# A decoder layer on one core: cross attention, its projection, the norm and the experts in one program, with a token chunk's later stages woven between the attention steps of the next chunk

## The chip, the core and the metric

The kernel runs on one core of one Trainium2 chip. Its engines work from queues of their own and meet only at semaphores: TensorE (PE, with its weight loads shown apart as PEld), VectorE (DVE), ScalarE (ACT), GpSimd (POOL), and SyncE (SP), which issues all DMAs here. Each queue is worked off in the order in which it was written. The metric is the device time in microseconds of one execution; the kernel before takes 1327.97 us (median of three runs, 1327.39 to 1332.73).

## The reference, cut to what matters

One decoder layer over 2048 tokens of width 256. After causal self attention and a layer norm come the stages that this change touches:

```python
qp = x @ Wq.T                               # 16 heads of 16
mem = kv[argmax(qp @ kv.T)]                 # each token picks one of 1601 context rows
mk, mv = split(mem @ Wkv.T)                 # one key, one value, shared by the heads
attn = softmax(qh @ mk.T / 4)               # over 2048 chosen rows, many of them equal
x = layernorm(x + (attn @ mv) @ Wc.T)
probs = sigmoid(x @ router_w.T)             # 8 experts, the best 2 are kept
combine = top-2 weights, normed to sum 1, 0 for the other experts
for e in range(8):                          # widths 256 x4, 512 x4
    y += combine[:, e] * (square(relu(x @ W1[e])) @ W2[e])
x = layernorm(x + y)
```

Equal rows are counted once, so that the keys of cross attention are at most 512 with this data: four tiles of 128 keys.

## The kernel before

The tokens stand in 16 tiles of 128 or four chunks of 512 (`NC` = 4, `C` = 512, `TC` = 4 tiles in each). The program is a row of blocks; no engine starts a block before all have ended the one ahead. The last three blocks are:

1. **Cross attention** (`attention("cross", ...)`). There are 16 units: a chunk and a group of four heads (`NG` = 4, `GH` = 4). A unit has 16 *pieces*: TensorE multiplies a query tile with all 512 keys (L527) into a bank of the ring `cross_max`, and VectorE takes the row maximum (L625). From them come the negated maxima (`cross_shift`), turned by TensorE (L532) and sent by a DMA into two rows of the query stack `stackx` (L463). Then come the unit's four *steps*, one for each tile of keys: scores in two pairs (L546), Exp (L592), and the sum over keys with the values (L557). Pieces of later units stand between the steps of the present one, where `schedule` puts them; each step is cut in thirds (after the first pair of scores, after the second, after the values). After a unit its sums are copied (L604), turned back (L536) and divided (L642, L644). The queries of a whole chunk, in 6 DMAs of 256 KB, are loaded at once (L453). The 8 banks of PSUM are 4 for scores, 1 for the output, 3 for the ring.
2. **Projection and norm** (`project_norm("n2", ...)`). For each chunk: turn the attention output (L758, copied at L787), multiply it by Wc (L776), add the residual (L810), mean and variance (L813, L815, L828, L830), the root on ScalarE (L834), normalise (L840), turn again (L758) and split into two fp32r parts (L787, L802). Beside that w2 is loaded and split into two parts (ScalarE L110, GpSimd L116).
3. **Experts.** First the router for all tokens, and its top 2 as a chain of small VectorE instructions (L1309 to L1328). Then for each chunk and expert the hidden tiles of 128 columns (function `hidden`, 6 matmuls of 512 columns each, into three banks `ph`), Relu (L1275) and Square (L1277) on ScalarE, the split on VectorE (L1298, L1300); and four output tiles `y`, each 6 or 12 matmuls of 256 columns per 256 or 512 of width, into four banks `py`, added to x at L1337. The hidden tiles of the next expert stand ahead of the outputs of this one. `product` (L92) makes three matmuls of each product, first by first, first by rest, rest by first. Then the last norm, and the output.

The line that keeps a ring in order, on TensorE, is the same before and after:

```python
if n >= SB:                  # SB = 3
    pe.wait_ge(*freed[n - SB])
```

## Time and profile before

| | us |
|---|---|
| median of three runs | 1327.97 |
| the profiled execution, its own time | 1334.47 |
| its span, first to last instruction | 1332.8 |
| loading the first queries of cross attention | 753.7 to 769.4 |
| cross attention | 769.4 to 987.6 |
| projection and norm, then the router | 987.6 to 1048.1 |
| experts up to the last matmul | 1048.1 to 1325.5 |
| last norm and output | 1325.5 to 1332.8 |

All times of instructions are those of the profiled execution, counted from the start of its span. A duration of a matmul holds the filling and draining of the array, so that a long row of matmuls is shorter than the sum of its single durations: the distance between the starts of like rows says what one costs. The same holds in a smaller measure for the other engines.

### The profile page before, as it was taken

How to read it: one execution, taken by the hardware profiler on the slowest of the kernel's cores; microseconds unless marked ns; L12 is line 12 of the kernel's file. 1: busy time of each engine (PE TensorE's matmuls, PEld its weight loads, DVE VectorE, ACT ScalarE, POOL GpSimd, SP SyncE). 2: the span in 40 equal slices, each digit the busy share in tenths (PEclk: the TensorE clock that was granted, in tenths of full speed). 3: DMA queues.
4: the chain of work that ended last, by engine and by line, in shares of the span. 5: the costliest groups of instructions: out<-in, count | busy, mean ns of one | idle time of the engine just before them, and what ended most of it. 6: DMA issues, size and time to landing. Idle time of an engine off the chain costs nothing. (4 is left out here: it accounts for less than half of the span.)

```text
span 1332.8 us, 18319 instructions
## 1 busy us (share of the span) xinstructions
PE 1171.6 (88%) x6937; PEld 642.9 (48%) x6937; DVE 955.4 (72%) x1875; ACT 640.6 (48%) x870; POOL 183.7 (14%) x167
## 2 busy tenths in 40 slices
PE   5864999999999999973899479999976799999997
PEld 2531233333333333243788213333334489999997
DVE  3564999898888887027699579999808466767675
ACT  1320246666766666841443115677653334444442
POOL 2223111021021100143000340500004000000000
PEclk9875799999999999986899659999987899999999
DMA  6215067920000000030110394200011000000000
GB/s 233 93 47 105 25 72 80 111 25 1 1 1 1 1 1 2 1 133 27 48 48 1 44 99 48 96 2 2 1 47 59 1 1 1 16 1 17 1 16 17
DMA packets 43927, 51.00 MB, mean 38 GB/s; under 512 B 7002, under 2 KB 39386, under 8 KB 43834
## 3 DMA queue, kind: packets, MB, share of 16 engines
q1 hardware_dynamic: 43834, 49.78, 19.4%
q8 instruction: 57, 0.93, 0.3%
q14 instruction: 36, 0.29, 0.1%
HBM read 37.64 MB, written 11.53 MB: 37 GB/s over the span
## 5 line engine op out<-in xcount | busy, mean ns | idle before, releaser
L625 DVE TENSOR_REDUCE self_piece_max<-self_max 128x1 f32<-128x512 f32 (+3 forms) x640 | 349.4, 604 | 52.4 <-PE self_max L527 25.4
L592 ACT ACTIVATE self_probs<-self_scores 128x1024 f32<-128x1024 f32 (+3 forms) x320 | 274.1, 896 | 192.9 <-PE self_scores L546 191.9
L527 PE MATMUL self_max<-stack_k,stack_q 96*128 96x512 bf16 (+3 forms) x640 | 209.6, 366 | 12.5 <-DMA stack_k<-kparts 6.3
L625 DVE TENSOR_REDUCE cross_piece_max<-cross_max 128x1 f32<-128x512 f32 x256 | 161.4, 684 | 28.4 <-PE cross_max L527 28.0
L546 PE MATMUL self_scores<-stack_q,stack_k 98*128 98x512 bf16 (+3 forms) x640 | 170.3, 350 | 4.3 <-DMA stack_q<-self_shift 3.0
L592 ACT ACTIVATE cross_probs<-cross_scores 128x1024 f32<-128x1024 f32 x128 | 124.7, 1022 | 93.5 <-PE cross_scores L546 91.6
L557 PE MATMUL self_out<-self_probs,V 128*17 128x512 f32 (+3 forms) x1280 | 148.7, 536 | 2.6 <-ACT self_probs L592 2.0
L527 PEld LDWEIGHTS self_max<-stack_k,stack_q 96*128 96x128 bf16 x640 | 62.2, 98 | 181.2 <-DVE self_piece_max L625 131.0
L1275 ACT ACTIVATE o_tok<-ph 128x512 f32<-128x512 f32 x96 | 57.5, 599 | 143.7 <-PE ph L92 137.5
L92 PE MATMUL py<-w_first,hid_first 128*128 128x256 f32 x384 | 108.9, 283 | 5.7 <-DVE x_sb L1337 5.7
L92 PE MATMUL py<-w_first,hid_rest 128*128 128x256 f32 x384 | 108.8, 283 | 0.0
L92 PE MATMUL py<-w_rest,hid_first 128*128 128x256 f32 x384 | 108.7, 283 | 0.0
L527 PE MATMUL cross_max<-kx_few,stackx 97*128 97x512 bf16 x256 | 95.9, 418 | 13.5 <-DMA stackx<-xparts 12.9
L494 POOL TENSOR_SCALAR_AFFINE_SELECT self_probs<-self_probs 128x512 f32<-128x512 f32 x64 | 40.6, 634 | 397.7 <-ACT self_probs L592 397.4
L1337 DVE SCALAR_TENSOR_TENSOR x_sb<-py,mix,x_sb 128x256 f32<-128x256 f32 x128 | 61.7, 482 | 36.2 <-PE py L92 29.7
L1298 DVE CAST hid_first<-o_tok 128x512 fp32r<-128x512 f32 x96 | 41.0, 427 | 64.0 <-ACT o_tok L1277 61.2
L546 PEld LDWEIGHTS self_scores<-stack_q,stack_k 98*128 98x128 bf16 x640 | 57.0, 99 | 53.8 <-ACT self_probs L592 16.3
L546 PE MATMUL cross_scores<-stackx,kx_few 99*128 99x512 bf16 x256 | 77.6, 387 | 3.2 <-DMA stackx<-cross_shift 3.1
L92 PEld LDWEIGHTS py<-w_first,hid_first 128*128 128x128 f32 x384 | 73.4, 191 | 7.4 <-issue 6.1
L92 PE MATMUL ph<-x2T_first,w_first 128*128 128x512 f32 x192 | 76.2, 397 | 0.0
L92 PE MATMUL ph<-x2T_rest,w_first 128*128 128x512 f32 x192 | 76.1, 396 | 0.0
L92 PE MATMUL ph<-x2T_first,w_rest 128*128 128x512 f32 x192 | 75.7, 394 | 0.0
(209 smaller groups left out, 1756.2 us busy)
## 6 DMA issues: line engine op xcount, KB each, us to landing
stack_q<-qparts SPq DMA_DIRECT2D x96, 64.0 KB, 8.3
stackx<-xparts SPq DMA_DIRECT2D x24, 256.0 KB, 10.9
stack_k<-kparts SPq DMA_DIRECT2D x18, 256.0 KB, 13.3
qparts<-parts SPq DMA_DIRECT2D x8, 384.0 KB, 2.5
kparts<-parts SPq DMA_DIRECT2D x8, 384.0 KB, 2.5
xparts<-xparts_sb SPq DMA_DIRECT2D x8, 384.0 KB, 2.7
cross_raw<-in_w SPq DMA_DIRECT2D x4, 768.0 KB, 5.4
n_raw<-in_w SPq DMA_DIRECT2D x6, 512.0 KB, 4.2
```

What stands on the lines that cost most here:

```text
L92: ins = nc.tensor.matmul(out, lhsT[a], rhs[b], start=first and n == 0, stop=last and n == len(terms) - 1)
L494: nc.gpsimd.affine_select(out=blk, in_=blk, compare_op=ALU.is_ge, fill=0.0, base=0, pattern=[[0, GH], [1, P]], channel_multiplier=-1).then ...
L527: mm = nc.tensor.matmul(slot[:, 0:pc["w"]], pc["lhsT"], pc["rhs"], start=True, stop=not pc["diag"])
L546: mm = nc.tensor.matmul(ps[:, j, st["off"]:C], st["keys"](j), st["queries"](j), start=True, stop=True)
L557: mm = nc.tensor.matmul(po[32 * j:32 * j + VW, st["off"]:C], st["values"](j), probs[:, i % 3, j, st["off"]:C], start=st["first"], stop=st[ ...
L592: nc.scalar.activation(probs[:, i % 3, 2 * pair:2 * pair + 2, st["off"]:C], ps[:, 2 * pair:2 * pair + 2, st["off"]:C], ACT.Exp, scale=SCAL ...
L625: nc.vector.tensor_reduce(piece_max[:, u % 2, pc["row"], pc["at"]:pc["at"] + 1], slot[:, 0:pc["w"]], AX.X, ALU.max).then_inc(side_read, 1)
L1275: nc.scalar.activation(relu[:, u % 3], ph[:, u % 3], ACT.Relu).then_inc(h_read, 1)
L1298: nc.vector.tensor_copy(hid[0][:, i % 2, w], square[:, u % 3]).then_inc(first_ready, 1)
L1337: nc.vector.scalar_tensor_tensor(out=x_sb[:, n], in0=py[:, y % 4, 0:D], scalar=mix[:, n, e:e + 1], in1=x_sb[:, n], op0=ALU.mult, op1=ALU.a ...
```

## The change

The three blocks become one. Its TensorE program is still the 64 attention steps, but `merge` puts items of the later stages behind the pieces in each third of a step, as soon as the chunk that they belong to has left attention:

- `back` (turn the attention output, 2 in a chunk), `proj` (2), `stats`, `norm`, `x2t` (turn and split the normed x, 2), `logit`, `ltr` and `mix` (router), `hid` (a hidden tile, 24), `rest` (its second part, on VectorE), `y` (an output tile, 32), `fstats` and `fnorm` (last norm).
- All that TensorE makes for these items goes through the one ring of three banks that the pieces use: the item waits until the third item before it has been read, by VectorE or by ScalarE.
- The weave gives each third of a step about 3,500 matmul columns, as long as items are ready; gaps counted in columns keep items apart (`gap`, in the list `norms`; 5 x 512 columns between `hid` and `rest`, 2 x 512 between `rest` and `y`). What is left after the last step follows in a row.
- Queries are loaded by unit (6 DMAs of 64 KB) into four slots (`SX` = 4), a unit two ahead, and from the fifth unit on only when the slot's last user is done.
- The hidden tile's first part is now written by ScalarE itself, with a second Square, and VectorE's cast goes. The root of the norms is a power of -0.5 on GpSimd. All of w1 and w2 is split on GpSimd, during the first chunk's attention.
- The router runs per chunk (4 tiles), not for all 16 tiles.

The diff, cut (`schedule` is only moved):

```diff
+SX = 4
+HR = 6
-            stackx = sb(stage, "stackx", [P, NC, H, C], BF16)
+            stackx = sb(tail, "stackx", [P, SX, GH, C], BF16)
+            banks = psum(tail, "banks", [P, 8, C])
+            ps, po, pm = banks[:, 0:GH], banks[:, GH], banks[:, GH + 1:8]
+            def merge(steps, works, first_of, before, thirds, diag_before):
+                norms = [[(("back", c, 0), 0), (("back", c, 1), 0), (("proj", c, 0), 4 * C), (("proj", c, 1), 0), (("stats", c), 2 * C),
+                          (("norm", c), 16 * C), (("x2t", c, 0), 3 * C), (("x2t", c, 1), 0), (("logit", c), 6 * C), (("ltr", c), 6 * C),
+                          (("mix", c), 3 * C)] for c in range(NC)]
...
+                    if rests and (force or now - when[("hid",) + rests[0]] >= 5 * C):
+                        give(("rest",) + rests.pop(0), slot)
...
+                pace = per_chunk * NC / (len(steps) * 3)
+                for i, step in enumerate(thirds):
+                    for k, given in enumerate(step):
+                        slot = list(given)
+                        credit = min(credit + pace, 4 * pace) if out_of[0] else 0
+                        while credit > 0:
+                            had = clock[0]
+                            if not pick(slot, False):
+                                break
+                            credit -= clock[0] - had
...
+                            if item[0] == "turn":
+                                sp.wait_ge(shift_ready, u + 1)
+                                for b, dst in enumerate(works[u]["shift_to"]):
+                                    sp.dma_start(dst, shift[:, u % 2, b]).then_inc(shift_in[u % 2], 16)
+                                if u + 2 < len(works):
+                                    if u + 2 >= SX:
+                                        sp.wait_ge(probs_used, first_of[u + 3 - SX])
+                                    load_unit(u + 2)
...
+                            elif kind == "hid":
+                                for k in range(KD):
+                                    mm = product(slot, [v[:, k, w * P:(w + 1) * P] for v in w1_sb], [xt[:, k] for xt in x2T], k == 0, k == KD - 1)
...
+                                nc.scalar.activation(relu[:, h % 2], slot, ACT.Relu).then_inc(act_read, 1)
+                                nc.scalar.activation(hid[0][:, h % HR], relu[:, h % 2], ACT.Square)
+                                nc.scalar.activation(relu[:, h % 2], relu[:, h % 2], ACT.Square).then_inc(square_ready, 1)
...
-    nc = bacc.Bacc("TRN2", target_bir_lowering=False, num_devices=1)
+    nc = bacc.Bacc("TRN2", target_bir_lowering=False, num_devices=1, dynamic_dma_scratch_size=1024)
```

**First place: TensorE's queue, the projection.** Before, this is the whole second block; `n_pt` and `n_py` are its banks, and no attention is left.

```order
L758 MATMUL n_pt<-ident,o_tok 128x128 x16
L776 MATMUL n_py<-n_w,n_oT 128x256 x8
L758 MATMUL n_pt<-ident,o_tok 128x128 x8
L776 MATMUL n_py<-n_w,n_oT 128x256 x8
L758 MATMUL n_pt<-ident,x_sb 128x128 x8
```

Now the same work of chunk 0 stands in the steps of unit 4, the first unit of chunk 1 (L1502 scores, L1441 pieces, L1511 values, L1453 `back`, L1460 `proj`; `banks` is all of PSUM).

```order
L1502 MATMUL banks<-stackx,kx_few 128x512 x2
L1441 MATMUL banks<-kx_few,stackx 128x512 x2
L1453 MATMUL banks<-ident,o_tok 128x128 x8
L1502 MATMUL banks<-stackx,kx_few 128x512 x2
L1441 MATMUL banks<-kx_few,stackx 128x512
L1460 MATMUL banks<-xwc_sb,o_tok 128x256 x4
L1511 MATMUL banks<-cross_probs,vx_few 17x512 x4
```

A matmul of the projection that had only its own kind around it has now the scores, pieces and values of another chunk on both sides.

**Second place: VectorE's queue, from the norm to the router.** Before, the router's chain works on 16 tiles at once, behind the split of the first hidden tiles (`hid_first`, `hid_rest`):

```order
L840 TENSOR_SCALAR x_sb<-x_sb,n_mv,n_rstd 128x256 x4
L802 TENSOR_TENSOR x2T_rest<-n_pt,x2T_first 128x512 x4
...
L1298 CAST hid_first<-o_tok 128x512
L1300 TENSOR_TENSOR hid_rest<-o_tok,hid_first 128x512
L1309 TENSOR_SCALAR gate<-gate 128x128
L1310 RECIPROCAL gate<-gate 128x128
L1312 MAX top<-gate 128x8 x16
L1315 MAX_INDEX at<-top,gate 128x8 x16
```

Now (chunk 0) norm, split and router stand among the maxima of pieces (L1623), which TensorE's ring waits for:

```order
L1623 TENSOR_REDUCE cross_piece_max<-banks 128x1 x5
L1670 TENSOR_SCALAR x_sb<-x_sb,norm_mv,norm_rstd 128x256 x4
L1623 TENSOR_REDUCE cross_piece_max<-banks 128x1
L1675 TENSOR_TENSOR x2T_rest<-banks,x2T_first 128x512 x2
L1703 TENSOR_TENSOR hid_rest<-o_tok,hid_first 128x512
...
L1680 TENSOR_SCALAR gate<-gate 128x32
L1681 RECIPROCAL gate<-gate 128x32
L1683 MAX top<-gate 128x8 x4
L1686 MAX_INDEX at<-top,gate 128x8 x4
```

The chain is on a quarter of the tiles and comes four times, with pieces, sums and output tiles queued behind it.

**Third place: SP's queue at the start of cross attention.** Before (16x16x512 is a chunk's part of the queries, `cross_shift` the maxima):

```order
L453 DMA stackx<-xparts 16x16x512 x12
L463 DMA stackx<-cross_shift 1x16x128 [waits cross_shift_ready]
L463 DMA stackx<-cross_shift 1x16x128
L453 DMA stackx<-xparts 16x16x512 x6
```

Now (16x4x512 is a unit's part; `o_tok` holds the raw weights):

```order
L1350 DMA stackx<-xparts 16x4x512 x6
L1355 DMA xwc_sb<-in_xwc 128x2x256
...
L1369 DMA stackx<-cross_shift 1x16x128 [waits cross_shift_ready]
L1369 DMA stackx<-cross_shift 1x16x128
L1350 DMA stackx<-xparts 16x4x512 [waits cross_probs_used]
L1350 DMA stackx<-xparts 16x4x512 x5
L1377 DMA o_tok<-in_w 128x6x256 [waits w_split] x2
```

The load of a unit's queries has moved from the start of the block to behind the maxima of the unit two before it, and from the fifth unit on behind a wait for the values of a step.

## Rows read from the trace of the kernel before

**Rows 1.** The page: the span.

```profile
span 1332.8 us, 18319 instructions
```

**Rows 2.** Windows: stretches, busy time and count by engine, TensorE clock, DMA.

```profile
753.68:769.43 15.75, 2.07 (x2) 0.50 (x2) 0.17 (x1) 1.28 (x1) 15.28 (x9) 0.50 1.06 116
799.65:965.07 165.42, 163.78 (x932) 51.92 (x932) 154.28 (x285) 112.23 (x122) 19.64 (x8) 1.00 0.16 30
965.07:987.64 22.57, 19.97 (x125) 4.77 (x124) 1.92 (x6) 17.51 (x20) 0.00 (x0) 1.00 0.01 2
987.64:1048.05 60.41, 39.05 (x170) 28.89 (x169) 34.21 (x82) 18.80 (x32) 14.33 (x7) 0.77 0.19 58
1048.05:1325.54 277.49, 271.81 (x1730) 247.25 (x1728) 182.55 (x421) 121.29 (x198) 0.00 (x0) 0.98 0.02 7
```

**Rows 3.** Timeline, 881 to 887: start, length, instruction of attention's steady steps.

```profile
883.11 0.39 PE L527 MATMUL cross_max<-kx_few,stackx 97*128 97x512 bf16 x1
883.33 0.60 PE L546 MATMUL cross_scores<-stackx,kx_few 99*128 99x512 bf16 x2
...
884.94 1.05 PE L557 MATMUL cross_out<-cross_probs,vx_few 128*17 128x512 f32 x8
885.93 0.39 PE L527 MATMUL cross_max<-kx_few,stackx 97*128 97x512 bf16 x1
```

**Rows 4.** Timeline of projection and norm, with idle time and releaser.

```profile
1000.26 1.04 PE L758 MATMUL n_pt<-ident,o_tok 128*128 128x128 f32 x8
1001.13 3.62 PE L776 MATMUL n_py<-n_w,n_oT 128*128 128x256 f32 x16
1004.59 1.04 PE L758 MATMUL n_pt<-ident,o_tok 128*128 128x128 f32 x8
1010.23 2.42 DVE L840 TENSOR_SCALAR x_sb<-x_sb,n_mv,n_rstd 128x256 f32<-128x256 f32 x1
1013.04 3.78 PE L776 MATMUL n_py<-n_w,n_oT 128*128 128x256 f32 x8 [5.69 <-DVE x_sb L810]
1018.22 1.89 PE L776 MATMUL n_py<-n_w,n_oT 128*128 128x256 f32 x8
1031.38 1.38 DVE L840 TENSOR_SCALAR x_sb<-x_sb,n_mv,n_rstd 128x256 f32<-128x256 f32 x4
```

**Rows 5.** The chain that ended last: matmuls of one chunk's experts.

```profile
1197.66 2.82 PE py L92 x24
1200.48 2.77 PE ph L92 x12
...
1264.44 2.82 PE py L92 x24
```

**Rows 6.** The page's groups: busy time, mean ns, idle before.

```profile
L625 DVE TENSOR_REDUCE cross_piece_max<-cross_max 128x1 f32<-128x512 f32 x256 | 161.4, 684 | 28.4 <-PE cross_max L527 28.0
L592 ACT ACTIVATE cross_probs<-cross_scores 128x1024 f32<-128x1024 f32 x128 | 124.7, 1022 | 93.5 <-PE cross_scores L546 91.6
L1337 DVE SCALAR_TENSOR_TENSOR x_sb<-py,mix,x_sb 128x256 f32<-128x256 f32 x128 | 61.7, 482 | 36.2 <-PE py L92 29.7
```

**Rows 7.** Timeline around the router's chain on VectorE, and one Square.

```profile
1058.34 0.69 DVE L1300 TENSOR_TENSOR hid_rest<-o_tok,hid_first 128x512 fp32r<-128x512 f32 x1
1058.95 0.22 DVE L1309 TENSOR_SCALAR gate<-gate 128x128 f32<-128x128 f32 x1
1060.37 0.63 ACT L1277 ACTIVATE o_tok<-o_tok 128x512 f32<-128x512 f32 x1
1065.81 0.29 DVE L1328 TENSOR_TENSOR mix<-mix,hot 128x128 f32<-128x128 f32 x1
```

**Rows 8.** DMA issues from 100 to 126: count, KB, median us to landing.

```profile
stack_q<-qparts SPq DMA_DIRECT2D x13, 64.0 KB, 3.1
```

**Rows 9.** Timeline, SP: the issue of six DMAs of queries.

```profile
782.39 3.04 SPq L453 DMA_DIRECT2D stackx<-xparts  x6
```

**Rows 10.** The page's DMA issues, of the whole span.

```profile
stack_q<-qparts SPq DMA_DIRECT2D x96, 64.0 KB, 8.3
```

More of the change, by code:

```diff
@@ L1171, in decoder_layer @@
[L1171 removed]
             w2_sb = [sb(tail, f"w2_{n}", [P, WT, D], F32R) for n in ("first", "rest")]
+            rw_raw = sb(tail, "rw_raw", [P, KD, E])
             rw_sb = [sb(tail, f"rw_{n}", [P, KD, E], F32R) for n in ("first", "rest")]
[L1174 to L1180 removed]
@@ new lines, in decoder_layer @@
+            shift = sb(tail, "cross_shift", [UR, 2, 2, P], BF16)
+            inverse = sb(tail, "cross_inverse", [P, 2, C // P, GH])
+            x2T = [sb(tail, f"x2T_{n}", [P, KD, C], F32R) for n in ("first", "rest")]
+            hid = [sb(tail, f"hid_{n}", [P, HR, C], F32R) for n in ("first", "rest")]
+            stats = sb(tail, "norm_stats", [P, NT, 6])
+            mv = sb(tail, "norm_mv", [P, NT, 2])
+            rstd = sb(tail, "norm_rstd", [P, NT])
+            minus_half = sb(tail, "minus_half", [P, TC])
@@ new lines, in plan @@
+            def plan(keys, vals, n):
+                steps, works = [], []
+                width = C if n == FEW else n // 4
+                for c in range(NC):
+                    for g in range(NG):
+                        u = c * NG + g
+                        here = stackx[:, u % SX]
+                        pieces = [dict(w=width, lhsT=here[0:KS + 1, j, q * P:(q + 1) * P],
+                                       rhs=keys[0:KS + 1, a * width:(a + 1) * width], row=j * GH + q, at=a)
+                                  for j in range(GH) for q in range(C // P) for a in range(n // width)]
+                        works.append(dict(pieces=pieces, shift_to=[
+                            here[KS + 1 + b:KS + 2 + b].rearrange("o h (n t) -> o (h n) t", t=P) for b in range(2)]))
+                        for t in range(n // P):
+                            steps.append(dict(unit=u, diag=0, first=t == 0, last=t == n // P - 1,
+                                              keys=lambda j, t=t: keys[0:KS + 3, t * P:(t + 1) * P],
+                                              queries=lambda j, u=u: stackx[0:KS + 3, u % SX, j, :],
+                                              values=lambda j, t=t: vals(t)))
+                return steps, works
```

729 lines of the change are left out of this document (511 added, 218 removed).

## Prediction

> **What bounds the kernel now.** I read the page for the span [rows 1], then the windows over the last three blocks with TensorE's share and clock in each [rows 2], then the timeline inside each window for what one step costs [rows 3, 4], and the chain that ended last for the experts [rows 5]. The reader is to see that TensorE is the bound almost everywhere, and so where it is not. From 799.65 to 965.07 it is busy 163.78 of 165.42 us at full clock. The experts' stretch is 271.81 of 277.49 us. Only 15.75 us of waiting for the first queries, the last steps of attention (22.57 us, where ScalarE is busy 17.51), and the 60.41 us of projection, norm and router, at a mean clock of 0.77, have room [rows 2]. The weave removes next to no work of TensorE, so it can only fill these holes; it can't speed up the rest. VectorE is busy 154.28 of the same 165.42 us: in pure attention it has no room either.
>
> **What can be gained.** All terms are waiting or slow clock that goes.
> - *First queries.* The wait is 15.75 us for twelve DMAs of 256 KB, of which the first six are needed [rows 2]. Now six of 64 KB are needed. Six are issued in 3.04 us [rows 9], so the last goes out near 2.5 us, and one lands 3.1 us later where the queue is short [rows 8]: about 6 us. Gain 9.5.
> - *Last steps of attention.* A score or a piece costs 0.22 us, the values of a step 0.99, a whole step 2.82 (883.11 to 885.93) [rows 3]. In the 22.57 us stand 32 scores, 10 values and 3 turned sums of about 0.5: 7.0 + 9.9 + 1.5 = 18.4. Gain 4.
> - *Projection, norm, router.* At full clock a bank of turns is 0.44 us (half of 1000.26 to 1001.13) and a chunk's projection 3.46 (1001.13 to 1004.59) [rows 4]. So 16 banks are 7.0, four projections 13.8, the router's 24 matmuls at 0.228 (a sixth of the 1.37 us of a hidden tile, two of which take 2.74 to 2.77 [rows 5]) 5.5, its turns near 1: 27.5 of 60.41 us [rows 2]. Gain 33.
> - *Experts.* One chunk takes 66.78 us (1197.66 to 1264.44) [rows 5], four take 267.1 of 277.49 [rows 2]: the difference is the slow clock at the start and the router's chain. Gain 10.4.
>
> Together 57 us: were nothing new waited for, the span would be 1276. VectorE's cast that goes, and ScalarE's second Square, lie beside TensorE. In 46 woven steps of near 7.5 us ScalarE has two Exps of 1.02 [rows 6] and one and a half hidden tiles of three instructions near 0.63 [rows 7], about 5.0 us; VectorE has four maxima of at most 0.68, 1.5 rests of 0.69, two outputs of 0.48 and the norms and router, about 5.5 [rows 6, 7]. Neither becomes the bound on average; what they cost, they cost as waits.
>
> **What is waited for anew.**
> - *Queries of units 4 to 7.* Each load waits for the values of the last step of the unit that had the slot, and the unit's first piece comes soon after in TensorE's queue. Counting the rows between the two at the prices of [rows 3], TensorE has 5.0 us of work for unit 4, 4.0 for unit 5, 1.5 for unit 6 and 0.7 for unit 7; from unit 8 on woven work covers it. A load takes 2.5 + 3.1, about 5.7 us [rows 8, 9]. Late are 0.7 + 1.7 + 4.2 + 5.0 = 11.6 us, and behind the piece everything on TensorE is queued. After a wait of 5.69 us the same eight matmuls took 3.78 us and not 1.89 [rows 4]; I add 1.8 for each of the two long waits. In all 15. Below: landing with the end of issue (3.0 us), 4 in all. Above: 8.3 us to landing, the median over all such DMAs [rows 10], most of them in long rows: 32, and clock. I stay by the short queue, since only six DMAs are under way.
> - *Norm, split and router, once a chunk.* `x2t` waits for the norm, 1.38 us for four tiles behind pieces on VectorE [rows 4], of which I let 1 us show. A hidden tile waits until both turned banks have been copied and split, 0.6 + 0.6 + 0.6 us behind the second bank, less the overlap: 1.5. The router's chain ran 7.15 us for 16 tiles (1058.95 to 1066.10) [rows 7]; for 4 tiles it lies between a quarter of that and all of it, and I take 3.4, since its 13 single instructions keep their number. Behind it are queued the maxima of two or three pieces, hence the ring: TensorE gets through two items of 1.4 us and waits 2. In all 4.5 a chunk, 18 for four. Below 0, above 8 a chunk.
> - *The ring elsewhere.* With narrow experts, four outputs of 0.7 us come together with two pieces, and VectorE's 0.6 and 0.5 us for each make a piece wait near 0.8 us; wide experts wait for ScalarE's three instructions a tile, near 0.3. Following the order at three places gave 2 us a chunk: 7.5. Below 0, above 25.
> - *The end.* The last two hidden tiles have nothing behind them but their own outputs: Relu and two Squares of the last tile but one, then of the last, then the rest, are 3 us after the last matmul. 3.
>
> **SBUF's ports.** The normalise of one tile took 2.42 us beside GpSimd's split, and 1.38 us for all four alone [rows 4]. I count 1.38, because ScalarE's copy for the first `back` waits for all splits. The Trainium skill says (SBUF — State Buffer, "Who interferes with whom") that VectorE in its 2-port modes and GpSimd lock each other out, while a VectorE instruction with at most one SBUF input outside these modes is free of GpSimd. By that rule the splits beside the first chunk's maxima cost nothing, and the norms would be long only where a split still ran: four tiles of 2.42 instead of 1.38, 8 us a chunk and 33 in all, if my reading of the wait is wrong. The trace agrees as far as it goes: GpSimd was busy 19.64 us in a stretch where TensorE lost 1.64 [rows 2].
>
> **The sum.** -57 + 15 + 18 + 7.5 + 3 = -13.5 us. The span goes from 1332.8 to about 1319. The profiled execution took 1334.47 us by its own time, 6.5 more than the median of the runs, 1327.97; taken off the median, the forecast is 1315.
>
> **Rivals.**
> 1. *The waits are hidden.* The ring and the chains cost a third of what I say, since TensorE's share in attention shows that three banks suffice at 92% of VectorE [rows 2], and loads land early. Against it: there no item was longer than 0.7 us. -57 + 5 + 10 + 3 + 3 leaves about -35: 1293.
> 2. *In-order queues hold each other (slower).* ScalarE's Exp of the next step stands behind three instructions of a hidden tile, that wait for TensorE; VectorE's maxima stand behind a `rest` that waits for ScalarE. One more wait of 0.5 us a step, about one Exp less its overlap, is 23 us over 46 steps: 1338. It decides from 0.3 us a step on. For it: before, ScalarE and VectorE were never woven with long items. Against it: their average room of 2 to 2.5 us a step.
> 3. *Loads land late.* At 8.3 us [rows 10] the four units wait 20 us longer, and the clock is lost more often: 1338.
> 4. *Nothing gained.* Half of rival 2 or of rival 3 brings the sum to zero: the holes are filled, and others open: 1327.
>
> **How the numbers follow.** Forecast 0.42, rival 1 0.20, rival 4 0.14, rival 2 0.14, rival 3 0.10. 0.5%, 6.6 us, is about what a measurement of this kernel tells from no change. Faster by more is the forecast and rival 1: 0.62. Within it rival 4: 0.14. Slower rivals 2 and 3: 0.24. The forecast's own range is 1304 to 1321. The range that leaves out no more than 2 in 10 goes into rival 1 and up to rivals 2 and 3: 1288 to 1340.
>
> **What would show it.** In the profile after, the first piece starts near 760. Pieces of units 6 and 7 follow idle time of 4 to 5 us ended by the DMA of queries; if it is 1 us or 10, that term is wrong. In each chunk TensorE waits near 2 us behind the router's chain and near 1.5 between `x2t` and the first hidden tile. Between these, a step of units 8 to 13 takes about 7.7 us; at 8.2 rival 2 holds. After the last step of attention, a chunk's experts take 67 to 70 us. The prediction is wrong if the clock falls in woven steps, or if ScalarE or VectorE is busy above 90% in them.

## The result: slower by 1%, and the profile after

The changed kernel takes 1342.82 us (median of 6 runs, 1338.93 to 1349.65), the kernel before, run beside it, 1329.37 us (1327.39 to 1332.73). The ratio is 1.0101, 95% interval [1.0071, 1.0131]. In a second set of runs it was 1341.39 against 1330.38 us, 1.0096 [1.0070, 1.0122] (the run e15 below). The forecast was 1315, the range ended at 1340.

The page of the changed kernel, span and the busy time of TensorE and VectorE (share of the span, instructions):

```profile
span 1340.1 us, 18687 instructions
...
PE 1182.8 (88%) x6943; PEld 640.1 (48%) x6943; DVE 906.4 (68%) x1799; ACT 673.7 (50%) x951; POOL 175.8 (13%) x167
```

The cross block starts at 750.0 us here (753.7 before), and its last matmul at 1331.6 (1325.4 before). The difference at its start need not come from the change: in a second profiled execution of the changed kernel (e15) it starts at 748.0, and in e8 and e1, which have the kernel before up to there, at 749.6 and 751.2. The windows of the joined block, cut where the work changes (length, then busy time and count of PE, PEld, DVE, ACT and POOL, then TensorE's clock):

```profile
750.00:768.60 18.60, 11.62 (x25) 3.50 (x25) 10.60 (x20) 1.28 (x1) 14.30 (x11) 0.50 0.44 142
768.60:800.00 31.40, 30.79 (x114) 7.90 (x115) 28.47 (x51) 12.53 (x13) 21.08 (x9) 0.74 0.44 138
800.00:858.00 58.00, 50.20 (x261) 18.05 (x260) 43.69 (x81) 28.55 (x32) 11.20 (x5) 0.94 0.17 50
858.00:886.00 28.00, 21.83 (x103) 11.14 (x101) 17.70 (x58) 14.93 (x23) 1.03 (x1) 0.88 0.06 15
886.00:985.00 99.00, 96.43 (x590) 64.77 (x591) 60.46 (x113) 58.78 (x87) 0.00 (x0) 1.00 0.05 13
985.00:1032.00 47.00, 39.80 (x202) 22.26 (x199) 31.40 (x91) 22.01 (x33) 2.14 (x2) 0.93 0.07 21
1032.00:1112.00 80.00, 79.79 (x487) 53.11 (x486) 49.70 (x91) 50.41 (x76) 0.00 (x0) 1.00 0.05 16
1112.00:1158.00 46.00, 41.06 (x232) 25.50 (x231) 32.27 (x93) 24.16 (x36) 2.01 (x2) 0.96 0.03 10
1158.00:1222.00 64.00, 64.00 (x395) 44.76 (x395) 24.37 (x48) 43.17 (x66) 0.00 (x0) 1.00 0.01 3
1222.00:1268.00 46.00, 38.36 (x231) 31.47 (x230) 23.40 (x77) 18.86 (x34) 2.32 (x2) 0.95 0.00 1
...
1318.00:1332.00 14.00, 10.77 (x78) 9.70 (x77) 3.92 (x8) 3.38 (x6) 0.00 (x0) 1.00 0.02 4
```

The reader is to see two things. In the woven stretches (886 to 985, 1032 to 1112, 1158 to 1222) TensorE is busy and at full clock, and VectorE is far from full (49.70 of 80 us). The holes stand at four places, at the start of each chunk's later stages: 858 to 886, 985 to 1032, 1112 to 1158, 1222 to 1268; below, these are called the chunk starts. TensorE is idle there for 6.2, 7.2, 4.9 and 7.6 us. In all four the clock is below full again (0.88, 0.93, 0.96, 0.95) after it had recovered.

Busy time alone hides part of the loss, because the record of a matmul is longer than the distance to the next one (0.28 us against 0.117 for an output matmul in a row), so that a gap of 0.1 or 0.2 us between two of them doesn't show as idle. Therefore I also took the distance from each matmul's start to the next one's and subtracted what its kind costs in a long row at full clock: 0.117 us an output matmul, 0.2275 hidden or router, 0.2155 piece or score, 0.216 projection, 0.109 a turn of 128 columns, 0.99 the values of a step. Summed over the three last blocks these prices make 475.6 us before and 476.2 after: the work is the same, and the rest of the time is lost, as idle time, as slow clock or as small gaps. In us:

```
                                                   before    after
start, up to 800 us                                  34.5     24.5
attention alone (before 800-964, after 800-858)      11.4     14.4
last steps of attention (before 964-988)              8.4      -
projection, norm, router (before 988-1048)           29.3      -
start of the experts and all behind (1048-1327)      11.6      -
the four chunk starts (11.3 + 13.6 + 9.3 + 11.9)      -       46.1
woven stretches and experts between them              -       16.3
the end, from 1318                                    -        3.4
sum                                                  95.2    104.7
```

Who TensorE waited for between 750 and 1340 us (total, times, longest):

```profile
PE banks L1441 <- issue: 7.3, 3, 3.8
PE banks L94 <- DVE hid_rest L1703: 7.2, 6, 3.1
PE banks L94 <- DVE x2T_rest L1675: 5.7, 4, 1.7
PE banks L1441 <- DVE cross_piece_max L1623: 5.0, 5, 2.0
PE banks L1466 <- DVE x_sb L1670: 3.5, 3, 1.5
```

The first row is the late queries. The profile names no releaser for it ("issue"), but SyncE's row says that the six DMAs go out from 838.88, each lands 2.2 us later (median), and the piece that needs them starts at 843.42.

```profile
838.88 2.65 SPq L1350 DMA_DIRECT2D stackx<-xparts  x6
...
843.42 1.01 PE L1441 MATMUL banks<-kx_few,stackx 97*128 97x512 bf16 x2 [3.85 <-issue]
```

The other four rows stand for the most part at the chunk starts; of the second row, 3.1 us are at the very end and 2.75 at the fourth start, where outputs wait for a hidden tile's second part. The start of the second chunk's later stages, in the timeline (L1660 statistics, L1670 normalise, L1466 turn, L1675 split, L1680 to L1699 the router's chain, L1623 maxima of pieces):

```profile
996.82 1.40 DVE L1660 BATCH_NORM_STATS2 norm_stats<-x_sb 128x6 f32<-128x256 f32 x4
...
998.98 1.13 POOL L1416 TENSOR_TENSOR norm_rstd<-norm_rstd,minus_half 128x4 f32<-128x4 f32 x1 [2.10 <-DVE norm_rstd L1665]
...
999.49 0.39 PE L1441 MATMUL banks<-kx_few,stackx 97*128 97x512 bf16 x1 [1.64 <-DVE cross_piece_max L1623]
...
1004.52 1.37 DVE L1670 TENSOR_SCALAR x_sb<-x_sb,norm_mv,norm_rstd 128x256 f32<-128x256 f32 x4
...
1006.04 1.17 PE L1466 MATMUL banks<-ident,x_sb 128*128 128x128 f32 x8 [1.49 <-DVE x_sb L1670]
...
1007.32 1.29 DVE L1675 TENSOR_TENSOR x2T_rest<-banks,x2T_first 128x512 fp32r<-128x512 f32 x2 [0.23 <-ACT x2T_first L1555]
1008.76 0.47 PE L94 MATMUL banks<-x2T_first,w_first 128*128 128x512 f32 x1 [1.55 <-DVE x2T_rest L1675]
...
1017.97 0.18 DVE L1680 TENSOR_SCALAR gate<-gate 128x32 f32<-128x32 f32 x1
...
1021.20 0.19 DVE L1699 TENSOR_TENSOR mix<-mix,hot 128x32 f32<-128x32 f32 x1
1021.43 0.69 DVE L1623 TENSOR_REDUCE cross_piece_max<-banks 128x1 f32<-128x512 f32 x1
...
1022.18 0.39 PE L1441 MATMUL banks<-kx_few,stackx 97*128 97x512 bf16 x1 [1.96 <-DVE cross_piece_max L1623]
```

TensorE waits four times within 23 us: 1.64 behind the statistics, 1.49 for the normalise, 1.55 for the split, 1.96 behind the router's chain, 6.6 us together. The rest of the 13.6 lost there is clock (a mean of 0.93 over 47 us is 3.3) and small gaps. The clock fell to half right behind two of these waits, from 1000.1 to 1003.5 and from 1024.0 to 1027.4.

### The profile page after: what moved, and what is told of

It is laid out like the page before. It is cut to its first block and busy times, and to the rows that moved or that the text cites. A ratio compares the mean times of both kernels' runs of the same rounds, so it can differ in the third digit from the quotient of the medians.

```text
span 1340.1 us, 18687 instructions
## 1 busy us (share of the span) xinstructions
PE 1182.8 (88%) x6943; PEld 640.1 (48%) x6943; DVE 906.4 (68%) x1799; ACT 673.7 (50%) x951; POOL 175.8 (13%) x167
## 5 line engine op out<-in xcount | busy, mean ns | idle before, releaser
L1623 DVE TENSOR_REDUCE cross_piece_max<-banks 128x1 f32<-128x512 f32 x256 | 165.0, 685 | 76.6 <-PE banks L1441 76.0
L1591 ACT ACTIVATE cross_probs<-banks 128x1024 f32<-128x1024 f32 x128 | 128.6, 1018 | 137.7 <-PE banks L1502 136.9
L94 PE MATMUL banks<-w_first,hid_first 128*128 128x256 f32 x384 | 119.9, 312 | 11.6 <-DVE hid_rest L1703 7.2
L1441 PE MATMUL banks<-kx_few,stackx 97*128 97x512 bf16 x256 | 97.2, 425 | 18.4 <-issue 7.3
L94 PE MATMUL banks<-w_rest,hid_first 128*128 128x256 f32 x384 | 109.0, 284 | 0.0
L94 PE MATMUL banks<-w_first,hid_rest 128*128 128x256 f32 x384 | 108.8, 283 | 0.0
L94 PE MATMUL banks<-x2T_first,w_first 128*128 128x512 f32 x192 | 85.3, 444 | 5.9 <-DVE x2T_rest L1675 5.7
L94 PEld LDWEIGHTS banks<-w_first,hid_first 128*128 128x128 f32 x384 | 74.0, 193 | 29.3 <-issue 12.1
L1502 PE MATMUL banks<-stackx,kx_few 99*128 99x512 bf16 x256 | 80.8, 398 | 3.0 <-DMA stackx<-cross_shift 3.0
L548 PEld LDWEIGHTS self_scores<-stack_q,stack_k 98*128 98x128 bf16 x640 | 57.0, 99 | 54.2 <-ACT self_probs L594 16.3
L94 PE MATMUL banks<-x2T_rest,w_first 128*128 128x512 f32 x192 | 77.0, 401 | 0.0
L94 PE MATMUL banks<-x2T_first,w_rest 128*128 128x512 f32 x192 | 76.9, 400 | 0.0
```

The costliest lines, as they stand in the source:

```text
L94: ins = nc.tensor.matmul(out, lhsT[a], rhs[b], start=first and n == 0, stop=last and n == len(terms) - 1)
L548: mm = nc.tensor.matmul(ps[:, j, st["off"]:C], st["keys"](j), st["queries"](j), start=True, stop=True)
L1441: mm = nc.tensor.matmul(slot[:, 0:pc["w"]], pc["lhsT"], pc["rhs"], start=True, stop=True)
L1502: mm = nc.tensor.matmul(ps[:, j], st["keys"](j), st["queries"](j), start=True, stop=True)
L1591: nc.scalar.activation(probs[:, i % 3, 2 * pair:2 * pair + 2], ps[:, 2 * pair:2 * pair + 2], ACT.Exp, scale=SCALE).then_inc(probs_ready, 1)
L1623: nc.vector.tensor_reduce(piece_max[:, u % 2, pc["row"], pc["at"]:pc["at"] + 1], slot[:, 0:pc["w"]], AX.X, ALU.max).then_inc(side_read, 1)
```

## The experiments

The expected times of the versions of the changed kernel that alter its order come from following its queues with the durations of the trace, without any cost for the clock. The runs were made in four sets, each on a chip of its own with the kernel before beside it (1330.4 to 1330.8 us); the ratios are to that one. Only e13 and e14 had the changed kernel beside them (e15). Where another run is compared with it, two differences are given, to its two medians, 1342.82 and 1341.39.

### Parts left out or given room, in the changed kernel

**e2, five slots for the queries.**

```diff
-SX = 4
+SX = 5
-            stats = sb(tail, "norm_stats", [P, NT, 6])
+            stats = sb(tail, "norm_stats", [P, TC, 6])
```

> The changed kernel with five query slots for four (and statistics kept for one chunk only, to make room), so that no load of units 4 to 7 waits for a unit that has just ended. In the changed kernel three such waits show, 7.3 us in all with the longest at 3.8 us, and TensorE then ran 6.8 us at half clock. Theory: both go, about 10 us: 1333, ratio to the kernel before 1.002, and no idle time above 1 us before the first piece of units 5 to 7. Rival: VectorE's maxima are what limits pure attention, so the pieces queue there in place of the load: gain under 4 us.

Measured: 1334.99 us, ratio 1.0036 [1.0021, 1.0051]; 6.4 to 7.8 us less than the changed kernel. The waits before the pieces of units 5 to 7 are gone. The term of late loads is real, and its size is 6 to 8 us, less than the 10 that I expected of the run.

**e3, no router's chain.**

```diff
-                                link(nc.vector.tensor_scalar_add(gate[:], gate[:], 1.0))
-                                link(nc.vector.reciprocal(gate[:], gate[:]))
...
-                                link(nc.vector.tensor_tensor(here, here, hot[:], ALU.add))
+                                link(nc.vector.tensor_copy(mix[:, c % 2], gate[:]))
```

> The changed kernel without the router's chain: in each chunk a single copy stands for the sigmoid's last steps, the top 2, the indices and the weights (about 3.45 us on VectorE in the changed kernel, 1017.97 to 1021.43), so the weights of the experts are not the reference's. Theory: the chains at the start of each chunk are what the weave costs, because VectorE's long rows of small instructions hold back three banks; this one shows as 2 to 3 us of TensorE's time a chunk: 8 to 12 us, 1332, ratio 1.003. Rival: the weave costs a little in every woven step (in-order queues hold each other), and the chain lies beside other work: gain under 4 us, 1339 to 1343.

Measured: 1328.63 us, ratio 0.9986 [0.9977, 0.9995]; 14.2 us less than the changed kernel's 1342.82, 12.8 less than its second median. That is 3.2 to 3.5 us a chunk, about the chain's 3.45 us on VectorE. But that is only the average: by the last table of this section the four chunk starts lose 5.3, 0.2, 1.4 and 5.6 us less. At the second one the wait behind the chain is gone, and the clock was lower instead. The same 38 us, first in this run, then in the changed kernel:

```profile
984.43:1022.43 38.00, 33.64 (x156) 18.43 (x156) 22.90 (x57) 17.72 (x26) 2.14 (x2) 0.82 0.08 25
988.04:1026.04 38.00, 30.88 (x155) 16.91 (x154) 26.64 (x82) 17.25 (x26) 2.14 (x2) 0.93 0.08 25
```

So the chain costs 13 to 14 us in all; how much of it is the waiting and how much the clock that falls with it, this run doesn't separate.

**e4, no norm between projection and experts** (the DVE instructions at L1660, L1663, L1665 and L1670 for this norm, and its power on GpSimd, left out).

```diff
                                 if kind == "stats":
-                                    dve.wait_ge(side_read, read_at[("proj", c, 1)])
+                                    return
...
+                                if kind == "norm":
+                                    dve.wait_ge(side_read, read_at[("proj", c, 1)])
+                                    nc.vector.memset(total[:], 0.0).then_inc(normed, TC)
+                                    return
```

> The changed kernel without the norm between projection and experts: no mean and variance, no power on GpSimd and no normalise (about 1.95 and 1.37 us of VectorE a chunk, with 1.1 us of GpSimd between); the turned x is the one that was not normed. The last norm stays. Theory: in a chunk TensorE waits 1.5 us for the normalise and 1.6 us for a piece's maximum behind the statistics, and loses clock behind it: 3 to 5 us a chunk, 12 to 20 in all, 1327, ratio 0.999. Rival as before: gain under 4 us.

Measured: 1334.48 us, ratio 1.0026 [1.0015, 1.0036]; 6.9 to 8.3 us less, about 2 a chunk. More than the rival's 4 and less than the 12 to 20 that I expected of it. The profiled execution was the fastest of the twelve (1329.37).

### The order of the weave

**e5, the router's chain in three items**, with maxima and outputs between them.

```diff
-                          (("mix", c), 3 * C)] for c in range(NC)]
+                          (("mixa", c), MGAP0), (("mixb", c), MGAP), (("mix", c), MGAP)] for c in range(NC)]
```

> The changed kernel with the router's chain cut into three items (sigmoid and maxima; indices and sum; weights), kept apart by gaps of 3, 2 and 2 times 512 columns, so that maxima and outputs stand between them on VectorE. Nothing else moves by intent. Without the chain the kernel took 1328.6, 14 us less. Theory: it is the chain's length in one row (3.45 us) and not its work that TensorE waits for, since three banks cover about two maxima: most of the wait goes and the work stays, 5 to 8 us: 1336, ratio 1.004. Rival: VectorE's work itself is short at that place, so cutting it changes nothing: 1341 to 1344.

Measured: 1345.80 us, ratio 1.0116 [1.0100, 1.0132]. No gain; here my theory fell. In its waits the maxima cost less (3.3 us for 5.0), but the outputs more (7.9 us for 3.3). The first output of a chunk needs the whole chain, which now takes longer from its start to its end: 7.1 us for the third chunk (1152.24 to 1159.38) in place of 3.4, with two maxima, a normalise and other work of VectorE in it, and TensorE waits 2.60 us behind it:

```profile
PE banks L96 <- DVE x_sb L1717: 7.9, 5, 2.7
...
PE banks L1443 <- DVE cross_piece_max L1625: 3.3, 5, 1.6
```

**e6, four numbers of the weave.**

```diff
-                          (("norm", c), 16 * C), (("x2t", c, 0), 3 * C), (("x2t", c, 1), 0), (("logit", c), 6 * C), (("ltr", c), 6 * C),
+                          (("norm", c), 16 * C), (("x2t", c, 0), 3 * C), (("x2t", c, 1), 2 * C), (("logit", c), 4 * C), (("ltr", c), 6 * C),
-                    if hidden and ("x2t", hidden[0][0], 1) in done and ahead < 2:
+                    if hidden and ("x2t", hidden[0][0], 1) in done and ahead < 2 and (force or now - when[("x2t", hidden[0][0], 1)] >= 2 * C):
-                pace = per_chunk * NC / (len(steps) * 3)
+                pace = 0.93 * per_chunk * NC / (len(steps) * 3)
```

> The changed kernel with four numbers of the weave changed and no instruction added or taken: pace 0.93 of the even pace, so that outputs of a chunk are left over when the next one is normed; 2 x 512 columns between the two turned banks and between the second and the first hidden tile; the router 4 x 512 behind the hidden tile and not 6. Theory: the waits at the start of a chunk stand there because nothing else is ready for TensorE (a whole step of unit 9 has none of the experts' work, the next one 19,456 columns): following the queues with the durations of the trace, 15 us go, 1328, ratio 0.998, with less half-clock time. Rival: the weave costs in every step, so that the gaps only shift it: 1339 to 1345.

Measured: 1323.03 us, ratio 0.9948 [0.9929, 0.9966]: 19.8 us less than the changed kernel, 18.4 less than its second median, with every instruction of it kept. So the time had gone into the order of the items, and not into the work or into the mixture as such; 16.3 us of it are less loss at the chunk starts (last table). The window of the second chunk's start, 40 us (compare 985 to 1032 above):

```profile
970.00:1010.00 40.00, 38.21 (x221) 22.72 (x217) 29.58 (x85) 22.20 (x33) 2.02 (x2) 1.00 0.07 24
```

**e13 and e14, pace and gaps apart; e15, the changed kernel again.**

> The changed kernel with the pace of the weave at 0.93 of the even pace, and no gap changed. Outputs of the chunk before are then still there while the next one waits for its norm (y(0,7,..) beside x2t(1,..)). Theory: other work ready at the chunk's start is the larger part of the 20 us of e6_gaps: 8 us less than the changed kernel, 1334, ratio 1.003. Rival: the distances between dependent items are the larger part: 1341 to 1344.

> The changed kernel with the gaps of e6_gaps (2 x 512 columns between the turned banks and ahead of the first hidden tile, router 4 x 512 behind) at the even pace. A step with 2,048 columns of woven work and then one with 20,480 stand there, as the gaps only hold back what nothing replaces. Theory: no gain, or a small loss, 1343 to 1346, ratio 1.010 to 1.012. Rival: the distances alone bring most of the 20 us: 1325 to 1332.

> The changed kernel once more beside the two, to give the differences on one chip: 1342 to 1344, ratio 1.010.

Measured: pace alone 1333.92 us, ratio 1.0027 [1.0015, 1.0038], 7.5 less than the 1341.39 of the changed kernel beside it; gaps alone 1339.16, ratio 1.0065 [1.0052, 1.0078], 2.2 less, little more than the 1.4 us between the two medians of the changed kernel; together (e6) 18.4. The pace did what I expected; of the gaps alone I had expected no gain or a small loss, 1343 to 1346. Neither the work at hand nor the distance is enough alone. What the planner puts into three steps of unit 9 (two pieces in each first third, and so on, left out) shows why:

```
changed kernel   step 36: nothing
                 step 37: norm(1) | x2t(1,0) x2t(1,1) hid logit rest hid ltr hid | rest mix hid
gaps alone       step 36: fstats(0) | norm(1) | x2t(1,0)
                 step 37: fnorm(0) x2t(1,1) | logit hid ltr hid rest mix hid rest hid | rest y(1,0,0) rest y(1,0,1)
pace and gaps    step 36: y(0,7,1) | norm(1) y(0,7,2) | x2t(1,0)
                 step 37: x2t(1,1) y(0,7,3) | fstats(0) logit | hid(1,0,0)
                 step 38: fnorm(0) ltr hid | rest rest mix hid | hid
```

At the even pace the first chunk's work has run out when the second one's norm is on its way, and the next step gets all that had been held back in one bunch (19,456 columns), a row in which each item needs the one before. With a slightly slower pace the last outputs of the chunk before, y(0,7,..), lie between those items, and the gaps have something to be filled with.

**e9, one block of woven items a step**, behind the values.

```diff
-                        while credit > 0:
+                        while credit > 0 and k == 2:
```

> The changed kernel with the woven items only in the last third of a step, behind the values, in place of all three thirds: the same work and pace, but only one block of woven items a step, so near four changes fewer a step between bf16 pieces or scores, values and fp32r products, near 180 in all. Following the queues with the durations of the trace the order alone is worth 14 us, since scores and Exp are no longer held back by woven items: 1329, ratio 0.999. Rival (each change of kind costs TensorE 0.05 to 0.1 us on top, which the changed kernel pays everywhere): another 9 to 18 us less, under 1320. Second rival (long blocks starve VectorE's maxima and ScalarE): 1343 or more.

Measured: 1328.81 us, ratio 0.9988 [0.9977, 1.0000], 12.6 to 14.0 us less than the changed kernel, what the order alone was expected to give. From the first chunk's hidden tiles to the end of attention TensorE changes between bf16, fp32 and fp32r about 168 times here and 285 times in the changed kernel, 117 fewer and not the 180 that I had reckoned; at 0.05 to 0.1 us each that would have been 6 to 12 us more. The rival that every woven step pays for its mixture falls. Nor did every step get cheaper because scores and Exp are held back less: counted as in the last table, about 12 us of the gain are at the chunk starts, most of it at the second (12 us lost before, 5 here) and the fourth (12 and 7), and about 3 us in the stretches behind them.

**e10, two banks in the ring** (in the version e7 below).

```diff
+SR = 2
-            ps, po, pm = banks[:, 0:GH], banks[:, GH], banks[:, GH + 1:8]
+            ps, po, pm = banks[:, 0:GH], banks[:, GH], banks[:, GH + 1:GH + 1 + SR]
```

> The version of e7_together with two banks in the ring for three, everything else alike. Theory: three banks are enough between the chains, but not more than enough: with two, every wide item waits for the reading of the one before the last, near 50 us more, 1360, ratio 1.022. Rival (the ring hardly counts, as the prediction's 7.5 us said): under 1325.

Measured: 1373.94 us, ratio 1.0326 [1.0312, 1.0340], 63 us more than e7 with three. Of these, 23.8 us are 67 waits for the maxima (3.8 us in e7):

```profile
PE banks L97 <- DVE cross_piece_max L1626: 15.1, 34, 1.4
PE banks L1444 <- DVE cross_piece_max L1626: 8.7, 33, 1.0
```

The other 40 us are for the most part no wait that the profile names. From start to start of the matmuls, 21 and 20 us are lost in the woven stretches behind the first and the second chunk start (889 to 995 and 1033 to 1143), 4 and 7 in e7; what each of these small gaps waited for stays open.

### The loads without the weave, in the kernel before

**e1 and e8, the first chunk's queries by unit, the other chunks' in DMAs of 256 KB**, in e1 issued two loads ahead, in e8 five.

```diff
-                                if u + 2 < len(loads):
-                                    load(u + 2)
+                                if u + ahead < len(loads):
+                                    load(u + ahead)
```

> The kernel before, with one part of the change alone: the queries of the first chunk are loaded by unit, 6 DMAs of 64 KB each, as four loads, two ahead. In the changed kernel the first piece starts 4.5 us after the cross block and not 15.7, and TensorE's excess over full-clock work up to 800 us is 24.5 us and not 34.5. Theory: this gain is real and stands alone, so the kernel comes out near 10 us faster than before: 1319, ratio 0.9925. Rival: the earlier start only lengthens the slow-clock stretch behind it, or the pieces of units 1 to 3 now wait for their loads: gain under 4 us, ratio above 0.997.

> The kernel before with the first chunk's queries by unit, as in e1_unit_loads, but with the load of the second chunk issued at the start too and every later one as early as in the kernel before. In e1_unit_loads TensorE waited 10.2 us at 803 and 11.1 us at 859 for pieces of the second and third chunk, whose DMAs of 256 KB had been issued later, and the run was 14 us slower than the kernel before. Theory: the gain at the start (first scores at 767 and not 784) is real and those waits are the whole loss: 1320, ratio 0.992. Rival: the second chunk's load beside the first units' takes the gain back: 1328 to 1331.

Measured: e1 1344.32 us, ratio 1.0100 [1.0085, 1.0114], a miss by 25 us; e8 1328.52, ratio 0.9984 [0.9974, 0.9994], a miss by 8. In e1 TensorE waited twice for DMAs. The first wait is for queries that had been asked for too late. The second is not for queries, as the expectation of e8 says, but for two small DMAs with maxima: they stand in SyncE's queue behind the raw weights, whose DMAs wait for GpSimd's splits:

```profile
813.85 0.59 PE L527 MATMUL cross_max<-kx_few,stackx 97*128 97x512 bf16 x1 [10.04 <-issue]
...
835.08 30.35 SPq L104 DMA_DIRECT2D cross_raw<-in_w  x4
865.48 2.40 SPq L463 DMA_DIRECT2D stackx<-cross_shift  x4
...
869.94 1.04 PE L546 MATMUL cross_scores<-stackx,kx_few 99*128 99x512 bf16 x2 [10.96 <-DMA stackx<-cross_shift]
```

In e8 the pieces of the first unit start as early (754.1), but the two DMAs of 4 KB with its maxima, issued behind 24 loads of 64 KB and six of 256 KB, took 11.4 us to land and not 1.7, so that the first scores start at 778.0 and not at 768.6 as in the changed kernel:

```profile
PE cross_scores L547 <- DMA stackx<-cross_shift: 12.8, 1, 12.8
```

The same wait is 3.0 us in the changed kernel.

**e11, all queries by unit.**

```diff
-                          for n, (a, _) in enumerate(PAIRS)] for c in range(NC)]
+                          for n, (a, _) in enumerate(PAIRS)] for c in range(NC) for g in range(NG)]
```

> The kernel before with the queries of all 16 units loaded by unit (6 DMAs of 64 KB each, two units ahead), as the changed kernel has them, and no weave. In e8_unit_loads_ahead a chunk's DMAs of 256 KB stood beside those of the first units, and the gain at the start was gone: 1328.5. Theory: with small loads alone the first scores come near 767 and no later piece waits: the loads are worth 8 to 10 us without the weave, 1321, ratio 0.993. Rival: as e8, 1327 to 1331.

Measured: 1328.08 us, ratio 0.9973 [0.9963, 0.9984], another miss: 2.5 us less than the kernel before. The start is as in the changed kernel (first piece 755.9, first scores 770.1), but the unit's load now stands in SyncE's queue behind the raw weights, whose DMAs wait for GpSimd's splits:

```profile
823.00 15.56 SPq L104 DMA_DIRECT2D cross_raw<-in_w  x4
838.61 1.14 SPq L463 DMA_DIRECT2D stackx<-cross_shift  x2
839.79 2.92 SPq L453 DMA_DIRECT2D stackx<-xparts  x6
...
845.55 1.01 PE L527 MATMUL cross_max<-kx_few,stackx 97*128 97x512 bf16 x2 [7.22 <-issue]
```

7.22 us and the clock that fell to half meanwhile (842.0 to 848.8) take back most of the gain. In e1, e8 and e11 the first piece comes 4.6 us after the block's start and not 15.7, but each run loses most of that, or more than that, again behind it; that the gain would stand alone is not shown.

### Together

**e7, five slots, the chain in three, and the gaps; e12, the same with the chain in one piece.**

> Five query slots, the router's chain in three items, and the gaps (pace 0.94; 6 x 512 columns between norm and first turn, 2 x 512 between the two turns and ahead of the first hidden tile; router 4 x 512 behind): all three of the runs apart. Theory: the terms add, since they stand at different places: 7 + 6 + 15 and a little clock, near 29 us below the changed kernel, 1313, ratio 0.987: the weave then beats the kernel before. Rival: what is freed at one place is waited for at the next (VectorE's maxima, the clock), and it stays above 1325.

> Five query slots and the gaps (pace 0.93; 12 x 512 columns ahead of the norm, 6 x 512 ahead of the first turn, 2 x 512 between the turns and ahead of the first hidden tile, router 4 x 512 behind), and the router's chain in one piece. e5_chain_in_three showed no gain from cutting the chain in the order as it was. Theory: cutting the chain is worth 4 to 5 us only where the gaps leave other work beside it: 1315, against 1310.5 of e7_together. Rival: the cut never mattered: 1310.

Measured: e7 1310.49 us, ratio 0.9853 [0.9837, 0.9868]; e12 1311.99, ratio 0.9865 [0.9848, 0.9882]. Both beat both kernels: e7 is 30.9 to 32.3 us below the changed kernel and about 20 below the one before. The cut of the chain is worth 1.5 us by the medians, and the two intervals overlap (the gaps differ slightly too): it isn't shown to be worth anything, and the 4 to 5 us that I expected of it are not there. Most of the gain is the slot and the order. In e7 the stretch over the second chunk's start, the steady one behind it and the third chunk's start read:

```profile
965.00:1010.00 45.00, 41.54 (x239) 25.05 (x238) 34.04 (x95) 23.80 (x36) 2.02 (x2) 1.00 0.11 30
1010.00:1090.00 80.00, 79.67 (x481) 51.35 (x481) 50.35 (x93) 51.01 (x76) 0.00 (x0) 1.00 0.04 11
1090.00:1118.00 28.00, 25.09 (x134) 14.33 (x132) 17.83 (x39) 12.34 (x17) 1.01 (x1) 0.94 0.00 1
```

The time lost in the 38 us around the first turned x of each chunk (from 18 before to 20 behind it, counted as in the table above) falls with the medians, but for neighbours. A single entry is one execution: in a second profile of the changed kernel (e15) the second start lost 1.3 us more and the fourth 1.3 less, with the same sum. In e5 the starts lose no more than in the changed kernel; what it lost on top is behind them, where its outputs wait.

```
                      four chunk starts    sum   median us
changed kernel        13.3 12.3 7.5 11.8   44.9   1342.8
e3 no router chain     8.0 12.1 6.1  6.2   32.4   1328.6
e4 no norm             8.7  8.9 7.4 10.0   35.0   1334.5
e5 chain in three     11.3 14.3 6.3 11.9   43.8   1345.8
e14 gaps alone        10.4 11.0 9.0 12.7   43.1   1339.2
e13 pace alone        10.6  9.4 7.9  8.1   36.0   1333.9
e6 pace and gaps       8.5  5.3 6.7  8.1   28.6   1323.0
e7 together            8.1  5.2 6.7  6.8   26.8   1310.5
```

From e6 to e7 the starts gain 1.8 us and the time 12.5: most of that is the fifth slot, ahead of the first start (13 us lost between 800 and there in e6, 4 in e7).

## Why the prediction was wrong

**What bounds the kernel, and what can be gained: right.** All the losses named went, 34.5 to 24.5 us at the start (forecast 9.5, got 10.0), 8.4 in the last steps (4), 29.3 in projection, norm and router (33), 11.6 in the experts (10.4). The 7.4 us that attention lost in its other steps, not counted in the forecast, went too: 66.7 for the 57 forecast.

**Queries of units 4 to 7: right, somewhat less.** I said 15. Units 6 and 7 waited 3.05 and 3.85 us, not 4.2 and 5.0, since the small DMAs took a median of 2.3 us and not 3.1; with the clock it was 14.4 less the 4 us that attention alone loses in 58 us (11.4 of 164), so 10.4. e2 gave 6.4 to 7.8 back.

**The failed step: "Norm, split and router, once a chunk ... In all 4.5 a chunk, 18 for four. Below 0, above 8 a chunk."** The time lost at the chunk starts measured 46.1 us, 11.5 a chunk, above its upper bound. TensorE is idle for 25.9 of them; the clock below full costs up to 10.8 (28 x 0.12 + 47 x 0.07 + 46 x 0.04 + 46 x 0.05); the rest are small gaps. The single waits that the term named were well forecast: near 1.5 between `x2t` and the first hidden tile (1.66, 1.55, 0.84 and 1.65 in the four chunks), 2 behind the router's chain (1.43, 1.96, 2.78 and 2.68, the last with the statistics of a last norm behind the chain; the chain took 3.45 for 3.4). Four things were missing. The statistics are a row on VectorE too (1.95 us, 1.64 of waiting). The normalise showed 1.49 and not 1. The clock fell behind these waits in each chunk but was priced only for the query loads. And I took the waits as if other items stood between them, because I followed the order at places where they did, not at the step that had no woven work and the one with 19,456 columns behind it. A fifth stands at the fourth start, 2.75 us behind a hidden tile's second part, which no term held at that place. e3 and e6 show it from two sides: leaving the router's chain out gives 3.2 to 3.5 us a chunk on average, and moving items without removing any gives 18 to 20 us.

**The ring elsewhere: inside its bounds.** Forecast 7.5, with bounds of 0 and 25; the woven stretches and the experts lost 16.3 us. That is twice the term, or 8.9 if the 7.4 of attention that went, and that the forecast had not counted, is set against it. e10 shows that three banks matter: with two, e7 took 63 us more.

**The end: right**, 3.4 us for 3.

**The sum.** With the measured sizes: -66.7 + 10.4 + 46.1 + 16.3 + 3.4 = +9.5, against the 9.8 us by which TensorE's part grew (580.8 from 571.0). The forecast's span of 1319 missed 1340.1 by 21: 28 in the failed step, less 5 in the other terms, less 2.6 outside of them (the block starts 3.7 us earlier, what follows the last matmul takes 8.5 us and not 7.4). The other 7 us of the miss are the step from the profiled execution to the median: I took 4 us off the span, because the kernel before had been profiled in an execution slower than its median; the changed kernel's median is 2.7 us above its profiled span.

**The rivals.** "In-order queues hold each other" gave nearly the right time (1338) for a reason that is not the right one. It priced half a us in every woven step. A step of units 8 to 13 does take 8.42 us (967.7 to 1169.8 for 24) and not 7.7, above the 8.2 that I had named as its mark; but of these 202.1 us only 29.0 are lost, and the chunk starts in it hold most of them: the mark was wrong, because the work itself is 7.2 us a step and the 7.7 had no room for the starts. From 1032 to 1112, ten steps, 4.1 us were lost: 0.4 a step of every kind of loss together, where attention alone had lost 0.2 (11.4 in 58 steps); the rival needed 0.5 more. e9 says the same: with one block a step the gain is that of the order, at the chunk starts. What is right in this rival is the mechanism at these places: behind the router's chain the maxima stood in VectorE's queue, and TensorE waited for them. "Loads land late" is not the case (2.3 us), nor is "the waits are hidden". Of the signs named, VectorE above 90% didn't show (62% from 1032 to 1112), the clock did fall, though at chunk starts, and the first piece came at 754.5, earlier than 760. The last chunk's experts took 80 us (1251.6 to 1331.6) and not 67 to 70, with 10.6 us lost, and with the last output of the chunk before and the router in it.

**SBUF's ports.** My reading held: the norms after the first chunk's splits took 1.37 us for four tiles, and GpSimd had nothing to do beside them but powers of 1.0 to 1.1 us.

## What to carry to other kernels

When work of one stage is woven into another, look first at where its dependent chain starts anew (norm, turn, split, router): there the planner must still hold independent work, so keep the pace a little below even and save the last outputs of the block before for that place. Here the gap numbers gave 2.2 us without such work, the work 7.5 without the gaps, and both 18.4. The Trainium skill says that kernels whose most contended engine changes may gain by interleaving those regimes (Perfetto Trace Analysis, "Optimization Strategy"); here the weave lost 1% in one order of the items, won 0.5% in another (e6), and 1.5% with a fifth query slot on top and the router's chain cut in three (e7). A small DMA that TensorE waits for must not stand behind a large load, nor behind one that waits for another engine.

## What the runs showed of the hardware

- Changing between bf16, fp32 and fp32r matmuls on TensorE costs little, if anything: from 1032 to 1112 it changes 71 times and all lost time is 4.1 us, so less than 0.06 us a change even if nothing else were lost; and e9, with about 117 fewer changes, gained 12.6 to 14.0 us, where following its order without any cost for changes had given 14.
- Two DMAs of 4 KB took 11.4 us (median) to land behind six loads of 256 KB and 24 of 64 KB in e8, and 1.7 in the changed kernel, where all that had been issued ahead of them had landed (no DMA traffic from 763 to 766).
- A DMA whose issue waits holds what stands behind it in SyncE's queue: four DMAs of raw weights, waiting for GpSimd's splits, took 30.35 us of the queue in e1 and 15.56 in e11, and TensorE then waited 10.96 and 7.22 us for the small DMAs and the queries behind them.
- GpSimd's power of a 128x4 tile took 1.0 to 1.1 us, as long as an Exp of 128x1024 on ScalarE (1.02).
